# Fetching weights, the second context and the cleared slots of a decoder layer later, with one bias row behind the constants

## The chip, the cores and the metric

The kernel runs on one core of a Trainium2 chip. The metric is the device time of one execution in microseconds. Everything is float32.

## The reference

One decoder layer over 8 batches of 112 tokens with 256 features, with a context of 375 rows per batch:

```python
x = _layernorm(x + attn(x, W1..W4, b1..b4))            # one head: softmax((xW1+b1)(xW2+b2)^T/16)(xW3+b3) W4 + b4
x = _layernorm(x + xattn(x, ctx, mask, ...))           # inside it, three sublayers, each with a residual and a norm:
#   ca = 16-head attention of x over ctx (scores + mask);  x = norm(ca @ co_w + co_b + x) * co_g + co_be
#   sa = 16-head attention of x over x;                    x = norm(sa @ so_w + so_b + x) * so_g + so_be
#   gelu(x @ fi_w + fi_b);                                 x = norm(. @ fo_w + fo_b + x) * fo_g + fo_be
x = _layernorm(x + ffn(x, centroids, gamma, beta, W1, b1, W2, b2))
#   each token goes to the expert (of 8) whose centroid fits best; norm, relu(h W1e^T + b1e) W2e^T + b2e, times alpha
```

## The kernel before, in words

The program is written by hand for five engines, with semaphores. A list, `STEPS`, gives the order of all stages; it is made once from a table of due times, and TensorE (`@block.tensor`), VectorE (`@block.vector`), ScalarE (`@block.scalar`) and GpSimd (`@block.gpsimd`) each walk through it and do their part of every stage. A stage is a pair of name and number. The names that matter here, for batch `u`:

- `aqk`, `as`, `at`, `av`, `ay`: the first attention (queries and keys from `xT_sb[:, u]`, scores, transposed probabilities, values, result). `aw` multiplies W3 by W4 once, so that the output projection is already in the values, and adds b4 to its row: VectorE's line 829, behind `b4_in`. TensorE's projections to a transposed layout are line 488, those to rows line 502.
- `ab`, `ax`: the norm behind it (VectorE, line 878, with the inverse deviation that GpSimd makes) and the transposition of its result (TensorE line 509; VectorE's copy out of PSUM, line 887, which counts up `out_free`).
- `ck`, `cv`: keys (line 495) and values (line 502) of the context; `cq`, `qk`, `cm`, `ct`, `pv`: cross attention's queries, scores, masked exponentials, transpositions, product with the values. VectorE's line 921 adds the mask.
- `sqk`, `sv` and so on: self attention. `f1` (line 656), `f2`: the feed-forward part. `al`, `sc`, `rk`: scattering the tokens to the experts' slots in `x_slots` and `x_more`. After `STEPS` come the experts' tiles (lines 701 to 736).

The steps are ordered by their due times, so for TensorE the first projection of batch 4, (`aqk`, 4), stands between (`ax`, 0) and (`ax`, 1), well before batch 0's first keys. Batch 0 reads `x_first_in`'s part of x, batches 1 to 3 `x_early_in`'s, batches 4 to 7 `x_late_in`'s.

The transfers do not stand in `STEPS`. SP (`@block.sync`) issues most of them in a loop over the batches: context `u`, mask `u`, and at certain `u` something else; from `u` = 2 on, SP first waits until the ring of two context buffers (`out_full`, of `ck` and `cv`) and of two masks (`scores_masked`) is free. In its queue stand also 14 stores of zeros, which clear the slots (`x_slots`, `x_more`), and the experts' weights (`moe`). ScalarE issues seven transfers before its first stage: the b4 row, broadcast; the weights of cross attention; nine more rows; the value biases; the weights of self attention (`wS`); and both feed-forward matrices (`fi_sb`, `fo_sb`). Each transfer raises a semaphore of its own by 16, and the stages wait for it where they first use the data: `w_self` at (`sqk`, 0), `w_ffn` at (`f1`, 0), `zero_in` at (`f1`, 0) and (`al`, 0). GpSimd adds the b4 row to all eight residuals (line 1229), then waits for the other rows and adds two pairs of them (lines 1232, 1233), before it begins with `STEPS`.

Of the kernel before, what the change touches and what calls it, by code (L numbers as in the profile page):

```python
# [12 lines left out]
B, S, D, KX = 8, 112, 256, 375  # L13
# [153 lines left out]
def number(increments):  # L167

    count, before = 0, {}
    for stage in STEPS:  # L170
        if stage[0] in increments:
            before[stage] = count
            count += increments[stage[0]]
    return before, count
# [3 lines left out]
OUT, N_OUT = number(dict(aw=4, aqk=2, av=1, ay=1, ax=1, ck=1, cv=1, cq=1, pv=1, cy=1, cx=1,  # L178
                         sqk=2, sv=1, sy=1, sx=1, f2=1, zx=1, sc=1, rk=1))
# [16 lines left out]
def decoder_layer(nc, xT, xrow, ctxT, mask, weights, fi, fo, cols, rows, vb, b2rows, moe, x_slots, x_more, out):  # L196
    ctx = ExitStack()
    with ctx:
# [3 lines left out]
        def sem(name):  # L202
            return ctx.enter_context(nc.semaphore(name))
# [7 lines left out]
        def take(words):  # L211
            top[0] += words
            assert top[0] <= ARENA, top
            return arena[:, top[0] - words:top[0]]
# [30 lines left out]
        wS = take(4 * C * D).rearrange("p (w c n) -> p w c n", w=4, c=C)  # L245
# [9 lines left out]
        fi_sb = take(C * F).rearrange("p (c f) -> p c f", c=C)  # L255
# [6 lines left out]
        fo_sb = take(FC * D).rearrange("p (f d) -> p f d", f=FC)  # L262
        spread = take(len(ROWS) * D).rearrange("p (r d) -> p r d", r=len(ROWS))
        R = {name: spread[0:S, i] for i, name in enumerate(ROWS)}
# [77 lines left out]
        def col(name, i=0, p=128):  # L342
# [3 lines left out]
        w_first, w_second, w_third, w_cross, w_self, w_ffn = [sem(n) for n in "w_first w_second w_third w_cross w_self w_ffn".split()]  # L346
        consts_in, b4_in, rows_in, v_bias_in, x_first_in, x_early_in, x_late_in, xrow_in, zero_in, moe_b2_in = [sem(n) for n in (
            "consts_in", "b4_in", "rows_in", "v_bias_in", "x_first_in", "x_early_in", "x_late_in", "xrow_in", "zero_in", "moe_b2_in")]
# [50 lines left out]
        def group(n):  # L399

            u, g = divmod(n, NG)
            return u, g, g // 2, g % 2

        def further_tiles(engine, experts=True):

            engine.wait_ge(more_placed, 3)
            loaded = [engine.value_load(tile_expert[0:1, c:c + 1], min_val=0, max_val=E - 1)
                      for c in (*range(EXTRA if experts else 0), EXTRA)]
            return loaded[-1], loaded[:-1]

        def when_used(engine, used, j):


            return engine.If(used > j - E) if j >= E else nullcontext()


        @block.sync
        def _(sp):
            sp.dma_start(xT_sb[:, 0:1], xT[:, 0:1]).then_inc(x_first_in, 16)
            sp.dma_start(wA[:, 0:1], weights[:, 0:1]).then_inc(w_first, 16)  # L420
            sp.dma_start(wA[:, 1:2], weights[:, 1:2]).then_inc(w_second, 16)
            sp.dma_start(consts[:, :], cols).then_inc(consts_in, 16)
            sp.dma_start(xT_sb[:, 1:4], xT[:, 1:4]).then_inc(x_early_in, 16)
            sp.dma_start(wA[:, 2:4], weights[:, 2:4]).then_inc(w_third, 16)
            sp.dma_start(resid[0:S], xrow).then_inc(xrow_in, 16)
            for u in range(B):
                if u >= 2:

                    sp.wait_ge(out_full, 1 + max(OUT["ck", C * (u - 1) - 1], OUT["cv", KC * (u - 1) - 1]))
                sp.dma_start(context[:, u % 2], ctxT[u]).then_inc(ctx_in[u % 2], 16)  # L430
                if u >= 2:

                    sp.wait_ge(scores_masked, H * (u - 1))
                sp.dma_start(masks[0:S, u % 2], mask[u:u + 1].to_broadcast([S, KX])).then_inc(mask_in[u % 2], 16)
                if u == 0:
                    sp.dma_start(xT_sb[:, 4:8], xT[:, 4:8]).then_inc(x_late_in, 16)
                if u == 1:

                    sp.wait_ge(setup, 18)
                    for t in range(TILES):  # L440
                        dst = x_slots[t * 128:(t + 1) * 128, :] if t < E else x_more[(t - E) * 128:(t - E + 1) * 128, :]
                        sp.dma_start(dst, zero[:, t % 2]).then_inc(zero_in, 16)
                if u == B - 2:

                    sp.wait_ge(out_free, OUT["ax", B - 1] + 1)
                    sp.dma_start(moe_w[:, 0], moe[0]).then_inc(moe_in[0], 16)
            sp.wait_ge(out_free, OUT["cy", B - 1] + 1)
            for e in range(1, 5):
                sp.dma_start(moe_w[:, e], moe[e]).then_inc(moe_in[e], 16)
            sp.wait_ge(out_free, OUT["sy", B - 1] + 1)  # L450
            for e in range(5, E):
                sp.dma_start(moe_w[:, e], moe[e]).then_inc(moe_in[e], 16)
            sp.wait_ge(hidden_ready, FIRST_PIECE[-1])
            sp.dma_start(b2_sb.rearrange("p e d -> p (e d)"), b2rows.to_broadcast([128, E * D])).then_inc(moe_b2_in, 16)
            sp.wait_ge(out_free, N_OUT)
            sp.wait_ge(scattered, 16 * B)
            used = None
            for t in range(TILES):
                if t == E:
                    used, _ = further_tiles(sp, experts=False)  # L460
                    sp.wait_ge(more_scattered, 16 * B)
                with when_used(sp, used, t):
                    if t >= 4:
                        sp.wait_ge(t_stats, t - 3)
                    src = x_slots[t * 128:(t + 1) * 128, :] if t < E else x_more[(t - E) * 128:(t - E + 1) * 128, :]
                    sp.dma_start(xs[:, t % 4], src).then_inc(tile_in[t % 4], 16)
# [628 lines left out]
        def _(act):  # L1095
            a = nc.scalar
            act.wait_ge(w_first, 16)
            act.dma_start(R["b4"], rows[:, 0:D].to_broadcast([S, D])).then_inc(b4_in, 16)
            act.dma_start(wC, weights[:, 4:8]).then_inc(w_cross, 16)
            act.dma_start(spread[0:S, 1:].rearrange("p r d -> p (r d)"), rows[:, D:].to_broadcast([S, (len(ROWS) - 1) * D]))\  # L1100
                .then_inc(rows_in, 16)
            act.dma_start(v_bias, vb.unsqueeze(0).to_broadcast([128, 2, D])).then_inc(v_bias_in, 16)
            act.dma_start(wS, weights[:, 8:12]).then_inc(w_self, 16)
            act.dma_start(fi_sb, fi).then_inc(w_ffn, 16)
            act.dma_start(fo_sb, fo).then_inc(w_ffn, 16)
            act.wait_ge(consts_in, 16)
            for stage, i in STEPS:
                kind = stage[0]
# [11 lines left out]
                elif stage == "cm":  # L1120
                    u, at = divmod(i, H)
# [3 lines left out]
                elif stage == "sm":  # L1125
                    u, g, m, h = group(i)
# [227 lines left out]
```

## Time and profile before

| | |
|---|---|
| median of 3 runs | 446.76 us (445.54 to 447.12) |
| profiled execution | 443.95 us, its span 442.1 us |
| TensorE matmul busy | 400.0 us, 90% of the span, 3676 instructions |
| VectorE busy | 273.1 us, 62% |
| ScalarE busy | 241.0 us, 55% |
| GpSimd busy | 127.3 us, 29% |
| mean granted TensorE clock | 0.969 of full |
| DMA | 37.87 MB, of it SP's queue 28.40, ScalarE's 5.60, GpSimd's 3.18 |

The page divides the span into 40 equal slices of 11 us, and gives the busy share of each engine in tenths (9 is 90% or more). A row of the timeline names when an instruction or a run of them began, how long it took in all, its engine and line, what it wrote and read, and in brackets how long the engine was idle just before and what ended that. A float32 matmul shows as two records. SPq and ACTq are the queues on which SP and ScalarE issue DMAs: the duration of such a row is that of the issue, and the time to landing stands in rows of its own.

### The profile page before, as it was taken

What the parts mean: (1) busy time and instruction counts of PE and PEld (TensorE: products, weight loads), DVE (VectorE), ACT (ScalarE), POOL (GpSimd) and SP (SyncE); (2) the same over time, 40 slices, a digit from 0 to 9 for tenths busy, and PEclk for the clock granted to TensorE, in tenths of its full rate; (3) what the DMA queues carried; (4) which work ended last, traced back from release to release, by engine and by line L of the source; (5) the groups of instructions that cost most, each with busy time, mean ns of one, the idle gap of its engine ahead of it and who ended that gap; (6) DMA issues with size and microseconds to landing.
All of it is one profiled execution on the core that took longest, in us unless ns stands there. A gap on an engine that the chain in (4) does not pass through costs nothing.

```text
span 442.1 us, 10512 instructions
## 1 busy us (share of the span) xinstructions
PE 400.0 (90%) x3676; PEld 336.1 (76%) x3676; DVE 273.1 (62%) x945; ACT 241.0 (55%) x822; POOL 127.3 (29%) x256
## 2 busy tenths in 40 slices
PE   5979999999999999999999999999996289998990
PEld 5756787878778778787887887877795189997990
DVE  5476776767676686776777517569677453435432
ACT  0202886588777978779789884855022023332420
POOL 5461102012023031040312205223536325222323
PEclk9999999999999999999999999999998579999996
DMA  7996120010010107000000006920864112111001
GB/s 215 274 362 194 37 51 3 17 36 17 2 36 17 36 2 237 7 18 1 4 0 2 4 1 242 429 93 1 332 262 137 43 49 76 36 37 38 27 13 37
DMA packets 10342, 37.87 MB, mean 86 GB/s; under 512 B 1441, under 2 KB 5777, under 8 KB 8401
## 3 DMA queue, kind: packets, MB, share of 16 engines
q1 hardware_dynamic: 8064, 28.40, 18.7%
q10 hardware_dynamic: 976, 5.60, 3.8%
q0 software_dynamic: 1248, 3.18, 2.2%
q8 instruction: 32, 0.52, 0.5%
q14 instruction: 22, 0.17, 0.1%
HBM read 32.13 MB, written 5.04 MB: 84 GB/s over the span
## 4 chain that ended last, share of the span: by engine, by line
PE 35%; DVE 8%; ACT 4%; issue 3%; POOL 2%; DMA 1%; DVEq 0%; POOLq 0%; ACTq 0%; SPq 0%
PE bank_scores L721 9%; PE bank_out L736 8%; PE bank_out L666 4%; PE bank_pt L656 4%; PE bank_pt L621 2%; PE bank_out L643 2%; PE bank_out L502 1%; ACT arena L1134 1%; DVE stats L797 1%; PE bank_out L488 1%; PE bank_scores L605 1%; DVE arena L921 1%; ACT arena L1123 1%; DVE arena L871 1%; ACT arena L1158 1%
## 5 line engine op out<-in xcount | busy, mean ns | idle before, releaser
L1143 ACT ACTIVATE arena<-bank_pt 125x448 f32<-125x448 f32 (+1 forms) x128 | 67.1, 545 | 37.2 <-PE bank_pt L621 35.2
L1123 ACT ACTIVATE arena<-arena,negmaxc 112x375 f32<-112x375 f32 x128 | 76.9, 604 | 17.2 <-DVE negmaxc L921 16.9
L921 DVE CUSTOM_DVE_ANT_0 arena<-bank_scores,arena 112x375 f32<-112x375 f32 x128 | 65.0, 542 | 19.8 <-PE bank_scores L611 15.3
L621 PE MATMUL bank_pt<-ident,arena 112*125 112x112 f32 (+1 forms) x512 | 74.1, 276 | 1.1 <-ACT arena L1143 0.6
L621 PEld LDWEIGHTS bank_pt<-ident,arena 112*125 112x125 f32 (+1 forms) x512 | 62.9, 175 | 12.7 <-ACT arena L1143 4.5
L502 PE MATMUL bank_out<-arena 128*112 128x256 f32 (+1 forms) x224 | 57.7, 386 | 0.4
L1221 POOL TENSOR_TENSOR vareps<-meanvar,scal 112x1 f32<-112x1 f32 (+1 forms) x50 | 9.9, 198 | 156.0 <-DVE meanvar L800 112.6
L1176 ACT ACTIVATE arena<-bank_scores,consts 128x128 f32<-128x128 f32 x80 | 22.8, 368 | 56.8 <-PE bank_scores L721 56.8
L1134 ACT ACTIVATE arena<-bank_scores,negmaxs 112x112 f32<-112x112 f32 x128 | 43.3, 353 | 6.3 <-DVE negmaxs L927 5.8
L488 PE MATMUL bank_out<-arena 128*128 128x112 f32 x320 | 41.9, 285 | 5.2 <-DMA arena<-weights 4.5
L502 PEld LDWEIGHTS bank_out<-arena 128*112 128x112 f32 (+1 forms) x224 | 37.2, 181 | 10.6 <-issue 2.2
L488 PEld LDWEIGHTS bank_out<-arena 128*128 128x128 f32 x320 | 39.9, 200 | 6.3 <-POOL scal L1192 4.5
L721 PE MATMUL bank_scores<-arena 128*128 128x128 f32 x320 | 39.5, 284 | 0.5 <-DVE arena L1047 0.5
L721 PEld LDWEIGHTS bank_scores<-arena 128*128 128x128 f32 x320 | 38.7, 201 | 0.9 <-issue 0.9
L736 PE MATMUL bank_out<-arena 128*128 128x256 f32 (+1 forms) x160 | 36.0, 379 | 0.0
L736 PEld LDWEIGHTS bank_out<-arena 128*128 128x128 f32 x160 | 29.7, 190 | 3.7
L605 PE MATMUL bank_scores<-arena 32*112 32x375 f32 x256 | 28.8, 518 | 1.8 <-issue 1.8
L666 PE MATMUL bank_out<-arena 128*112 128x256 f32 x128 | 29.2, 381 | 0.4 <-DVE arena L871 0.4
L656 PE MATMUL bank_pt<-arena 128*128 128x224 f32 (+1 forms) x160 | 28.6, 327 | 0.6 <-ACT arena L1158 0.5
L643 PE MATMUL bank_out<-arena 125*32 125x112 f32 (+1 forms) x1024 | 28.7, 260 | 0.5 <-DVE gap L957 0.4
L1224 POOL TENSOR_TENSOR rstd<-vareps,scal 112x1 f32<-112x1 f32 (+1 forms) x50 | 28.0, 560 | 3.9
L1158 ACT ACTIVATE arena<-bank_pt,consts 128x224 f32<-128x224 f32 (+1 forms) x40 | 13.4, 409 | 24.9 <-PE bank_pt L656 24.9
(156 smaller groups left out, 637.2 us busy)
## 6 DMA issues: line engine op xcount, KB each, us to landing
arena<-moe SPq DMA_DIRECT2D x8, 2048.0 KB, 12.7
arena<-ctxT SPq DMA_DIRECT2D x8, 375.0 KB, 3.1
arena<-weights ACTq DMA_DIRECT2D x2, 1024.0 KB, 19.2
arena<-mask SPq DMA_DIRECT2D x8, 164.1 KB, 3.3
x_slots<-arena SPq DMA_DIRECT2D x8, 130.0 KB, 26.3
arena<-x_slots SPq DMA_DIRECT2D x8, 130.0 KB, 2.1
arena<-fi ACTq DMA_DIRECT2D x1, 1024.0 KB, 25.2
arena<-fo ACTq DMA_DIRECT2D x1, 1024.0 KB, 28.1
```

Of the source, the lines that this page charges most:

```text
L488: last = mm(dst[:, m * S:(m + 1) * S], w[:, k, m * 128:(m + 1) * 128], src[:, k], start=k == 0, stop=k == C - 1)
L502: last = mm(dst[0:rows, 0:D], src[:, k], w[:, k], start=k == 0, stop=k == C - 1)
L621: last = nc.tensor.transpose(dst[0:kp, j * S:(j + 1) * S], probs[0:S, (n % 2) * HG + j, c * kp:(c + 1) * kp], ident[0:S, 0:S])
L643: last = mm(dst[32 * j:32 * j + 32, at:at + S], v[:, c, cols:cols + 32], probsT[0:kp, (2 * h + p) % RT, c, j * S:(j + 1) * S], start=p == ...
L656: last = mm(dst[:, at * n:(at + 1) * n], fi_sb[:, k, f * 128:(f + 1) * 128], x3T[:, k, batches[0] * S:batches[0] * S + n], start=k == 0, s ...
L666: last = mm(dst[0:S, 0:D], hiddenT[:, q % 2, f, j * S:(j + 1) * S], fo_sb[:, f], start=f == 0, stop=f == FC - 1)
L721: last = mm(bank[2 * (j % 2) + f // 4][:, f % 4 * 128:(f % 4 + 1) * 128], w1[:, c, f * 128:(f + 1) * 128], xsT[:, j % 2, c], start=c == 0, ...
L736: last = mm(bank[6 + j % 2][:, 0:D], hidT[:, j % 2, f], w2[:, f], start=f == 0, stop=f == FC - 1)
L921: v.tensor_tensor_reduce(out=probsC[0:S, i % (2 * HG)], in0=score_bank[j][0:S, 0:KX], in1=masks[0:S, u % 2], scale=-1.0, scalar=3.0e38, op ...
L1123: a.activation(probsC[0:S, i % (2 * HG)], probsC[0:S, i % (2 * HG)], ACT.Exp, bias=negmax["c"][0:S, u, at:at + 1], scale=-1.0, accum_out=s ...
L1134: a.activation(probsS[0:S, (i % 2) * HG + j], score_bank[j][0:S, SELF_AT:SELF_AT + S], ACT.Exp, bias=negmax["s"][0:S, u, at:at + 1], accum ...
L1143: a.activation(probsT[0:kp, n % RT, c], pt_bank[PT[stage, i] % RP][0:kp, 0:HG * S], ACT.Copy).then_inc(pt_free, 1)
```

## The change

The order of the stages and the sizes stay. Only SP's and ScalarE's DMA issues move:

```diff
             sp.dma_start(consts[:, :], cols).then_inc(consts_in, 16)
+            sp.dma_start(R["b4"], rows[:, 0:D].to_broadcast([S, D])).then_inc(b4_in, 16)
             sp.dma_start(xT_sb[:, 1:4], xT[:, 1:4]).then_inc(x_early_in, 16)
             sp.dma_start(wA[:, 2:4], weights[:, 2:4]).then_inc(w_third, 16)
             sp.dma_start(resid[0:S], xrow).then_inc(xrow_in, 16)
             for u in range(B):
+                if u == 1:
+
+                    sp.wait_ge(out_free, OUT["ax", 0] + 1)
                 if u >= 2:
 
                     sp.wait_ge(out_full, 1 + max(OUT["ck", C * (u - 1) - 1], OUT["cv", KC * (u - 1) - 1]))
...
                 sp.dma_start(masks[0:S, u % 2], mask[u:u + 1].to_broadcast([S, KX])).then_inc(mask_in[u % 2], 16)
-                if u == 0:
+                if u == 1:
                     sp.dma_start(xT_sb[:, 4:8], xT[:, 4:8]).then_inc(x_late_in, 16)
-                if u == 1:
+                    sp.dma_start(wS, weights[:, 8:12]).then_inc(w_self, 16)
+                if u == 2:
 
                     sp.wait_ge(setup, 18)
                     for t in range(TILES):
                         dst = x_slots[t * 128:(t + 1) * 128, :] if t < E else x_more[(t - E) * 128:(t - E + 1) * 128, :]
                         sp.dma_start(dst, zero[:, t % 2]).then_inc(zero_in, 16)
+                if u == 3:
+                    sp.dma_start(fi_sb, fi).then_inc(w_ffn, 16)
+                    sp.dma_start(fo_sb, fo).then_inc(w_ffn, 16)
...
             act.wait_ge(w_first, 16)
-            act.dma_start(R["b4"], rows[:, 0:D].to_broadcast([S, D])).then_inc(b4_in, 16)
             act.dma_start(wC, weights[:, 4:8]).then_inc(w_cross, 16)
...
             act.dma_start(v_bias, vb.unsqueeze(0).to_broadcast([128, 2, D])).then_inc(v_bias_in, 16)
-            act.dma_start(wS, weights[:, 8:12]).then_inc(w_self, 16)
-            act.dma_start(fi_sb, fi).then_inc(w_ffn, 16)
-            act.dma_start(fo_sb, fo).then_inc(w_ffn, 16)
             act.wait_ge(consts_in, 16)
```

SP's queue, from the eighth of its transfers on, before (`ctxT` is a context, `xT` of 896 elements the x of batches 4 to 7, both in the big tile `arena`):

```order
L430 DMA arena<-ctxT 128x750
L434 DMA arena<-mask 112x375
L436 DMA arena<-xT 128x896
L430 DMA arena<-ctxT 128x750
L434 DMA arena<-mask 112x375
L442 DMA x_slots<-arena 128x260 [waits setup]
L442 DMA x_slots<-arena 128x260 x7
L442 DMA x_more<-arena 128x260 x6
L430 DMA arena<-ctxT 128x750 [waits out_full]
```

and the same place of the change:

```order
L434 DMA arena<-ctxT 128x750
L438 DMA arena<-mask 112x375
L434 DMA arena<-ctxT 128x750 [waits out_free]
L438 DMA arena<-mask 112x375
L440 DMA arena<-xT 128x896
L441 DMA arena<-weights 128x2048
L434 DMA arena<-ctxT 128x750 [waits out_full]
L438 DMA arena<-mask 112x375 [waits scores_masked]
L447 DMA x_slots<-arena 128x260 [waits setup]
L447 DMA x_slots<-arena 128x260 x7
L447 DMA x_more<-arena 128x260 x6
```

The x of batches 4 to 7 has moved behind the second context and mask, and these stand behind a wait for `out_free`, of which nothing stood there before; the stores have moved behind the third context and mask.

ScalarE's queue before its first exponential (`rows` of 256 elements is b4), before:

```order
L1098 DMA arena<-rows 112x256 [waits w_first]
L1099 DMA arena<-weights 128x2048
L1100 DMA arena<-rows 112x2304
L1102 DMA arena<-vb 128x512
L1103 DMA arena<-weights 128x2048
L1104 DMA arena<-fi 128x2048
L1105 DMA arena<-fo 128x2048
```

and of the change:

```order
L1106 DMA arena<-weights 128x2048 [waits w_first]
L1107 DMA arena<-rows 112x2304
L1109 DMA arena<-vb 128x512
```

Four transfers have gone from it to SP. TensorE's rows are the same before and after; where it meets the moved x, they read:

```order
L509 MATMUL bank_out<-ident,xrows 128x112 [waits out_free,norm_done]
L509 MATMUL bank_out<-ident,xrows 128x112
L488 MATMUL bank_out<-arena 128x112 [waits out_free,x_late_in]
L488 MATMUL bank_out<-arena 128x112 x3
L488 MATMUL bank_out<-arena 128x112 [waits out_free]
L488 MATMUL bank_out<-arena 128x112 x3
```

The first two are (`ax`, 0), whose copy SP now waits for, the others (`aqk`, 4).

## Rows read from the trace of the kernel before

**Rows 1.** The page's 40 slices: TensorE's and the DMA engines' busy tenths.

```profile
PE   5979999999999999999999999999996289998990
...
DMA  7996120010010107000000006920864112111001
```

**Rows 2.** Stretches: length, busy time of each engine, granted clock, DMA share, GB/s.

```profile
20.00:30.00 10.00, 7.66 (x46) 5.49 (x44) 7.25 (x23) 0.86 (x4) 7.26 (x14) 1.00 1.01 319
```

**Rows 3.** TensorE's waits up to 60 us: total, times, longest.

```profile
PE bank_out L488 <- DMA arena<-weights: 4.5, 1, 4.5
```

**Rows 4.** Timeline of GpSimd: start, duration, what, idle time before.

```profile
17.44 5.51 POOL L1229 TENSOR_TENSOR arena<-arena 112x256 f32<-112x256 f32 x8 [10.96 <-DVE minus_centroids L830]
24.98 0.72 POOL L1232 TENSOR_TENSOR arena<-arena 112x256 f32<-112x256 f32 x1 [2.02 <-DMA arena<-rows]
```

**Rows 5.** Timeline of VectorE: first norm of batch 0, copy of its transposition.

```profile
27.84 0.41 DVE L878 TENSOR_SCALAR xrows<-arena,meanvar,rstd 112x256 f32<-112x256 f32 x1
...
30.34 0.38 DVE L887 COPY arena<-bank_out 128x224 f32<-128x224 f32 x1
```

**Rows 6.** SP's issues on the timeline; then issues by size, with us to landing.

```profile
0.80 0.39 SPq L419 DMA_DIRECT2D arena<-xT  x1
...
2.66 0.43 SPq L423 DMA_DIRECT2D arena<-xT  x1
...
7.90 13.37 SPq L442 DMA_DIRECT2D x_slots<-arena  x7
...
arena<-xT SPq DMA_DIRECT2D x1, 448.0 KB, 20.7
arena<-xT SPq DMA_DIRECT2D x1, 336.0 KB, 4.4
```

**Rows 7.** Timeline of TensorE: sixteen projection records with and without DMA traffic.

```profile
20.65 2.04 PE L488 MATMUL bank_out<-arena 128*128 128x112 f32 x16
...
58.95 1.95 PE L488 MATMUL bank_out<-arena 128*128 128x112 f32 x16
```

**Rows 8.** Timeline of TensorE: the first projections of batch 4.

```profile
29.59 2.33 PE L488 MATMUL bank_out<-arena 128*128 128x112 f32 x16 [0.68 <-DVE arena L868]
```

**Rows 9.** The context's issue and landing; SP's later timeline; a single large transfer.

```profile
L430 SPq DMA_DIRECT2D arena<-ctxT x8: 328/330/949, 4.1 to 174.7; - x8
...
DMA to landing us min/median/max: 2.8/3.1/23.1
...
56.97 0.82 SPq L430 DMA_DIRECT2D arena<-ctxT  x1
79.06 0.33 SPq L434 DMA_DIRECT2D arena<-mask  x1
...
arena<-b2rows SPq DMA_DIRECT2D x1, 1024.0 KB, 5.1
```

**Rows 10.** Around idle times of TensorE: timeline, stretches (columns as rows 2), chain.

```profile
339.85 0.54 PE L680 MATMUL bank_out<-chosen,ones 112*112 112x8 f32 x2 [2.19 <-DVE chosen L969]
...
352.00:356.00 4.00, 1.18 (x5) 0.72 (x5) 1.80 (x7) 0.00 (x0) 0.00 (x0) 0.50 0.51 133
4.50:8.40 3.90, 3.90 (x18) 3.90 (x19) 1.29 (x4) 0.00 (x0) 1.91 (x13) 1.00 0.87 260
...
355.94 5.88 PE L721 MATMUL bank_scores<-arena 128*128 128x128 f32 x32 [0.49 <-DVE arena L1047]
...
362.03 3.57 PE bank_scores L721 x32
```

**Rows 11.** First uses on TensorE: self attention, fourth and fifth context, feed-forward.

```profile
79.85 1.95 PE L488 MATMUL bank_out<-arena 128*128 128x112 f32 x16
97.90 1.44 PE L495 MATMUL bank_out<-arena 128*128 128x375 f32 x4
129.74 1.43 PE L495 MATMUL bank_out<-arena 128*128 128x375 f32 x4
...
L656 PE MATMUL bank_pt<-arena x160: 275/352/457, 252.7 to 333.4; 128*128 128x224 f32 x96, 128*128 128x112 f32 x64
```

## The prediction

> **What bounds the kernel now.** I read the page's slices first [rows 1]: TensorE is at nine tenths or more from the fourth slice to the thirty-first, so the matmul queue sets the pace, except at the start and around 350 us. The DMA engines are nearly full in the first three slices and mostly idle afterwards, up to the late ones. Second the stretch in which both meet, 20 to 30 us [rows 2]: DMA share 1.01 at 319 GB/s, and TensorE idle for 2.3 of 10 us. Does the full DMA system hold the matmuls up? The waits of TensorE answer it [rows 3]: the only DMA that it waited for up to 60 us is the first weight, 4.5 us, and that one is issued before any that the change moves. The other waits there are for VectorE and ScalarE, the latency chain of the first attention. On GpSimd one wait ends with a DMA, 2.02 us for the broadcast rows [rows 4].
>
> **What could be gained.** The crowd at the start is hardly on the path. With the rows in sooner, GpSimd's two additions would follow its eight residual additions at 22.95 (17.44 + 5.51) instead of 24.98 [rows 4]. But what VectorE takes from GpSimd next, the first normalisation at 27.84, shows no idle time before it [rows 5]: VectorE came from other work. I count 0. b4 is moved ahead and away from ScalarE's crowd, so it lands sooner; nobody waited for it: 0. It pushes the second to fourth inputs back by one issue, 0.43 us, from 2.66 + 4.4 = 7.1 to 7.5 us [rows 6]. They are needed by the seventeenth projection matmul; 18 ran in the first 3.9 us from 4.50 [rows 10], so at 8.0: 0 again, though by only 0.5. ScalarE loses four issues that lie before its first exponential, which waits for VectorE: 0. Only slowing by traffic is left. Sixteen projection matmuls took 2.04 us in the crowd and 1.95 with an idle DMA system [rows 7]; 4.6% of the 26 us up to 30.7 is 1.2 us at the most, on a chain that is mostly latency. I take 0.
>
> **What is lost: batch 4's input.** The fetch of x for batches 4 to 7 landed 20.7 us after its issue [rows 6], in time: TensorE didn't wait for it [rows 3]. Now SP first waits for VectorE's copy of the first transposed batch (ax of batch 0), which runs from 30.34 to 30.72 [rows 5]; then it issues the second context, its mask, and only then this x. TensorE's order is unchanged, and in it the first projection of batch 4 stands directly behind that same transposition: it started at 29.59 [rows 8]. The transfer is now asked for after it is needed.
>
> When does it land? An issue takes 0.33 us [rows 9]: context at 30.8, mask 31.1, x 31.5. With 375 and 164 KB ahead of its own 448 KB, 987 KB must move. Lower end: x as if alone, 31.5 plus the 3.1 us of a context of 375 KB [rows 9], 34.6. Upper end: the pace at which the start moved its first 1,033 KB, 6.3 us from 0.80 to 7.1 [rows 6], so 6.0 us: 36.8. Nearest is a single transfer of 1,024 KB on an idle system, 5.1 us [rows 9]; scaled 5.0, so 35.8. The stall at batch 4's projection is 35.8 - 29.59 = **6.2 us**, between 5.0 and 7.2. Everything behind it on TensorE waits, among it the first keys, queries and scores, and with them VectorE, ScalarE and GpSimd, which have nothing else to do meanwhile but two normalisations. As TensorE then runs without gaps for 28 slices [rows 1], nothing takes the shift back.
>
> In sentences apart: the Trainium skill, page "DMA: Bandwidth & Descriptors", section "Anatomy of one DMA — SWDGE (gpsimd) path", gives one DMA a fixed 2.0 us plus its bytes over 436 GB/s; by that, 987 KB take an estimated 4.3 us, the stall is 5.5, and the sum below 7.1 instead of 7.8. The same rule makes 4.4 us of the 1,024 KB that took 5.1 here [rows 9]; the row decides.
>
> **What is lost: the clock.** After 2.19 us of idling TensorE's matmuls of eight columns took 0.54 us a pair; the granted clock from 352 to 356 is 0.50, which is 1.2 GHz, and the next 32 matmuls took 5.88 us where 32 like them took 3.57 later: 2.3 us for one restart [rows 10]. At the start of the kernel the granted clock reads 1.00, yet 18 matmuls took 3.9 us where 16 take 1.95 later, so 1.7 us more than such 18 would [rows 7, 10]. A stall of 6.2 us behind a stretch with 2.3 us of idling in ten [rows 2] should drop the clock to 1.2 GHz too. I take **2.1 us**, nearer to the restart after an idle time; the ends are 0 and 2.3.
>
> **Given back.** Batch 4's sixteen matmuls are now spread over 2.33 us instead of 1.95 and wait 0.68 for VectorE [rows 8]. In a stall VectorE catches up, and at half the clock it has longer for its part. At most 0.7, at least 0.3; I take **0.5**.
>
> **The other moves.** The second context lands before x and is used after it: 0. Self-attention weights: 1,024 KB behind x, in by about 40; first used at 79.85 [rows 11]: 0. The 14 clearing stores move from 7.90 to behind the third mask, where the next issue stood at 56.97, with the shift 65; beside other traffic the first seven took 13.37 us to issue [rows 6], so fourteen 26.7. Behind them in SP's queue stands the fourth context: issued by 92, landed by 95, needed at 97.90 + 8 = 106 [rows 9, 11]: hidden with 11 us to spare. Both feed-forward weights go behind the fourth mask, issued at 79.06 before [rows 9]; their 2,048 KB take about twice 5.1 us, to 98 with the shift. The fifth context, behind them, is used at 129.74 and the feed-forward begins at 252.7 [rows 11]. All 0. A cover that fails there would show as a DMA wait of TensorE at one of these places.
>
> **Sum.** 6.2 + 2.1 - 0.5 = **+7.8 us**. The profiled execution took 443.95 (span 442.1, 1.85 around it), 2.8 below the median of the three runs, 446.76. On its own time that makes 451.8; on the median, **454.6**. The mechanism's own bounds are 5.0 + 1.7 - 0.7 = 6.0 and 7.2 + 2.3 - 0.3 = 9.2, so 452.8 to 456.0.
>
> **Rivals.** That the change doesn't do what it says is out: the rows of the four compute engines are the same in the same order, but for ScalarE's DMA issues.
> - *The clock stays up.* For it: 2.3 us of gaps between 20 and 30 us left it at 1.00 [rows 2]. Against: the pair behind 2.19 us of idling [rows 10]. It gives 6.2 - 0.4 = 5.8: 452.6.
> - *The self weights share the engines with x.* If the 1,024 KB issued behind x move beside it, x lands with all 2,011 KB; at 2.0 us per 649 KB (5.1 less 3.1, [rows 9]) that is 3.1 us later. +10.9: 457.7. Against: the second to fourth inputs landed 4.4 us after their issue, though over a megabyte was queued right behind [rows 6].
> - *The stores hold the fourth context.* It decides if the fourteen take more than 37 us; at 3 us each, 42, the fourth keys wait 5 more: +13: 460. Against: 1.9 each in the worst company [rows 6].
> - *The other side: relief at the start.* The copy that releases SP comes earlier, because rows and traffic no longer hold anybody up. Only what pulls that copy forward counts, and all of it does; from 30.7 it would have to move to 22.9 to make up for 7.8. The rows allow 2.0 [rows 4] and 1.2, so +4.6: 451.4. For the sign to turn, most of the first attention's latency would have to be waiting for DMA behind the names of other engines; then, with 9 us of relief, 445.6.
>
> **How the numbers follow.** Forecast 0.78 (454.6); clock stays up 0.09 (452.6); weights share 0.05; stores 0.03; relief that cancels the loss 0.05, of which 0.03 ends within the bound and 0.02 beyond. A measurement of this kernel can tell about 0.5%, 2.2 us, from no change. So slower 0.95, same 0.03, faster 0.02. The range goes from 450.5, under the quiet clock with partial relief, to 458.0, above the shared weights. The stores and full relief are left out, 8 in 100, and some of the forecast's own tail: three runs alone span 1.6 us.
>
> **What would show it.** The waits of TensorE up to 60 us have a second DMA entry, for x, of 5 to 7 us, at the first projection behind the first transposition; the sixteen matmuls of batch 4 take about 4 us instead of 2.33; SP's next issue after the first mask stands at about 30.8; no later wait of TensorE ends with a DMA. GpSimd's wait for the rows is gone, and nothing is faster for it. I am wrong if there is no such wait, or if it is there and the end moves by less than 4 us: then later stages had slack that I don't see.

## The result, and the profile of the changed kernel

The changed kernel takes 458.99 us (median of 4, 458.41 to 464.32), the kernel before beside it 446.94 (445.54 to 447.52): ratio 1.0301, 95% interval 1.0221 to 1.0381. That is 12.0 us slower where 7.8 had been forecast, and 1.0 us above the top of the range. The profiled execution took 459.31 us with a span of 457.4. The ratios, here and below, go by means and not by medians: they leave out runs more than 1.5% above the fastest of their kernel, and here the run of 464.32 us raises the mean.

The page's slices of the changed kernel, to be set beside [rows 1]; the line between is the granted TensorE clock in tenths. One slice is 11.4 us:

```profile
PE   4964999999999999999999899999997288998990
...
PEclk9895999999999999999999999999999569999997
DMA  7905017061001011500000003940674122010001
```

The crowd of transfers is gone after the second slice, and the fourth slice, busy to nine tenths before, is busy to four tenths and at half the clock. From the fifth on, the picture is the old one. TensorE's waits say by whom, where [rows 3] had one line:

```profile
PE bank_out L496 <- DMA arena<-xT: 10.6, 2, 8.7
...
PE bank_out L496 <- DMA arena<-weights: 4.6, 1, 4.6
```

Two waits for x instead of the one that was forecast. TensorE's timeline has both in place (L496 is L488 of before):

```profile
4.57 3.64 PE L496 MATMUL bank_out<-arena 128*128 128x112 f32 x16 [4.57 <-DMA arena<-weights]
10.07 2.58 PE L496 MATMUL bank_out<-arena 128*128 128x112 f32 x16 [1.86 <-DMA arena<-xT]
...
31.69 0.35 PE L517 MATMUL bank_out<-ident,xrows 112*128 112x112 f32 x2
40.80 3.75 PE L496 MATMUL bank_out<-arena 128*128 128x112 f32 x16 [8.75 <-DMA arena<-xT]
44.34 0.58 PE L517 MATMUL bank_out<-ident,xrows 112*128 112x112 f32 x2
...
45.53 1.48 PE L503 MATMUL bank_out<-arena 128*128 128x375 f32 x4
```

At 10.07, batch 1's projection starts 1.9 us after the end of batch 0's. At 40.80 it is batch 4's projection, which stood at 29.59 [rows 8]. Before, batches 0 and 1 made one unbroken run of 32 records, and the first keys stood at 32.79:

```profile
4.50 5.80 PE L488 MATMUL bank_out<-arena 128*128 128x112 f32 x32 [4.50 <-DMA arena<-weights]
...
32.79 1.50 PE L495 MATMUL bank_out<-arena 128*128 128x375 f32 x4
```

SP's queue of the change and the landings behind it:

```profile
3.13 0.43 SPq L424 DMA_DIRECT2D arena<-xT  x1
...
33.88 0.33 SPq L434 DMA_DIRECT2D arena<-ctxT  x1
34.25 0.43 SPq L438 DMA_DIRECT2D arena<-mask  x1
34.72 0.43 SPq L440 DMA_DIRECT2D arena<-xT  x1
35.20 0.43 SPq L441 DMA_DIRECT2D arena<-weights  x1
...
arena<-weights SPq DMA_DIRECT2D x1, 1024.0 KB, 8.0
...
arena<-xT SPq DMA_DIRECT2D x1, 448.0 KB, 6.0
arena<-xT SPq DMA_DIRECT2D x1, 336.0 KB, 6.9
```

x of batches 1 to 3 landed 6.9 us after an issue at 3.13, so at 10.0; in [rows 6] it was 2.66 + 4.4 = 7.1. x of batches 4 to 7 landed at 34.72 + 6.0 = 40.7. VectorE's copy of (`ax`, 0), for which SP waits, came 3.1 us later than the 30.34 of [rows 5]:

```profile
33.47 0.38 DVE L895 COPY arena<-bank_out 128x224 f32<-128x224 f32 x1
```

The clock, in stretches (length, busy times, granted clock, DMA share, GB/s):

```profile
36.00:40.00 4.00, 0.00 (x0) 0.00 (x0) 0.00 (x0) 0.00 (x0) 0.00 (x0) 0.50 0.91 241
40.00:44.00 4.00, 3.20 (x15) 3.20 (x16) 0.67 (x2) 0.00 (x0) 0.00 (x0) 0.50 0.47 198
44.00:48.00 4.00, 3.80 (x20) 2.83 (x20) 2.11 (x6) 0.00 (x0) 0.00 (x0) 0.81 0.01 2
```

From 36 to 40 us no engine does anything, and TensorE resumes at a granted clock of 0.50, which is 1.2 GHz. GpSimd no longer waits for the rows, where it had waited 2.02 us [rows 4], and nothing behind it is sooner for that: VectorE's first norm began at 30.97 us, 3.1 later than before like everything around it.

```profile
26.03 0.72 POOL L1236 TENSOR_TENSOR arena<-arena 112x256 f32<-112x256 f32 x1
```

Against before, the first keys start at 45.53 instead of 32.79, 12.7 us later, and this distance stays: the feed-forward matmuls

```profile
L664 PE MATMUL bank_pt<-arena x160: 274/352/457, 265.4 to 346.1; 128*128 128x224 f32 x96, 128*128 128x112 f32 x64
```

run from 265.4 to 346.1, where they ran from 252.7 to 333.4 [rows 11]. The two spans differ by 15.3 us; the last 2.6 arise among the experts' tiles, in a gap of 1.01 us and smaller ones for which the profile shows no cause. The medians differ by 12.0 only.

### The profile page after: what moved, and what is told of

It reads as the page before. It is cut to its first block, busy times and chain, and to the rows that moved or that the text cites. A ratio compares the mean times of both kernels' runs of the same rounds, so it can differ in the third digit from the quotient of the medians.

```text
span 457.4 us, 10512 instructions
## 1 busy us (share of the span) xinstructions
PE 403.8 (88%) x3676; PEld 339.7 (74%) x3676; DVE 273.4 (60%) x945; ACT 240.8 (53%) x822; POOL 127.4 (28%) x256
## 4 chain that ended last, share of the span: by engine, by line
PE 33%; DVE 7%; ACT 4%; issue 3%; DMA 2%; POOL 2%; DVEq 0%; POOLq 0%; ACTq 0%; SPq 0%
PE bank_scores L729 9%; PE bank_out L744 7%; PE bank_out L674 4%; PE bank_pt L664 4%; PE bank_pt L629 2%; PE bank_out L651 2%; PE bank_out L510 1%; ACT arena L1138 1%; DVE stats L805 1%; PE bank_out L496 1%; PE bank_scores L613 1%; DVE arena L929 1%; ACT arena L1127 1%; DVE arena L879 1%; DMA out<-arena,tile_token 1%
## 5 line engine op out<-in xcount | busy, mean ns | idle before, releaser
L929 DVE CUSTOM_DVE_ANT_0 arena<-bank_scores,arena 112x375 f32<-112x375 f32 x128 | 65.1, 543 | 19.8 <-PE bank_scores L619 15.3
L496 PE MATMUL bank_out<-arena 128*128 128x112 f32 x320 | 44.2, 295 | 15.2 <-DMA arena<-xT 10.6
L496 PEld LDWEIGHTS bank_out<-arena 128*128 128x128 f32 x320 | 42.0, 210 | 16.2 <-DMA arena<-xT 11.0
L510 PEld LDWEIGHTS bank_out<-arena 128*112 128x112 f32 (+1 forms) x224 | 37.3, 181 | 10.6 <-issue 2.4
L744 PEld LDWEIGHTS bank_out<-arena 128*128 128x128 f32 x160 | 29.7, 190 | 3.6
```

The costliest lines, as they stand in the source:

```text
L496: last = mm(dst[:, m * S:(m + 1) * S], w[:, k, m * 128:(m + 1) * 128], src[:, k], start=k == 0, stop=k == C - 1)
L510: last = mm(dst[0:rows, 0:D], src[:, k], w[:, k], start=k == 0, stop=k == C - 1)
L744: last = mm(bank[6 + j % 2][:, 0:D], hidT[:, j % 2, f], w2[:, f], start=f == 0, stop=f == FC - 1)
L929: v.tensor_tensor_reduce(out=probsC[0:S, i % (2 * HG)], in0=score_bank[j][0:S, 0:KX], in1=masks[0:S, u % 2], scale=-1.0, scalar=3.0e38, op ...
```

## The experiments

All times are medians beside the kernel before on the same chip. Before itself took 444.7 to 448.4 us there, so I compare distances to before. Every row and every landing comes from one execution of its kernel. "x early" is x of batches 1 to 3, "x late" that of batches 4 to 7. Waits are in us.

**Taking the two losses apart.** `b4_only` is the kernel before with

```diff
+            sp.dma_start(R["b4"], rows[:, 0:D].to_broadcast([S, D])).then_inc(b4_in, 16)
             sp.dma_start(xT_sb[:, 1:4], xT[:, 1:4]).then_inc(x_early_in, 16)
...
-            act.dma_start(R["b4"], rows[:, 0:D].to_broadcast([S, D])).then_inc(b4_in, 16)
```

> The kernel before with only the b4 row moved: from ScalarE's queue to SP's, behind the constants and ahead of x of batches 1 to 3. Theory A (the move alone delays x of batches 1 to 3 from 7.1 to about 10.0 us after the start, and everything behind it): 3.1 us slower than before, TensorE waits 1.9 us for x at its second batch, (ax, 0) is copied at about 33.5. Theory B (the prediction: the move only costs one issue, 0.43 us, and is covered; what came late in the change came from the other moves): within 0.5 us of before.

`after_b4_back` is the change with these lines undone.

> The change, but b4 again as the first transfer of ScalarE. Theory A: 3.1 us faster than the change, the copy of (ax, 0) at 30.3, the stall for x of batches 4 to 7 as long as before at 8 us or a little more. Theory B: no faster than the change.

`after_x_back` is the change with x late where it was:

```diff
-                if u == 1:
+                if u == 0:
                     sp.dma_start(xT_sb[:, 4:8], xT[:, 4:8]).then_inc(x_late_in, 16)
+                if u == 1:
                     sp.dma_start(wS, weights[:, 8:12]).then_inc(w_self, 16)
```

> The change, but x of batches 4 to 7 again behind the first mask, ahead of SP's wait. Theory A (the stall of 8.7 us at batch 4 and the slow clock behind it are 9.5 us of the 12.7): 9.5 us faster than the change, some 3.1 over before. Rival (later moves cost something too, the rest of the 15 us between the two profiled executions): 5 us or more over before.

`after_both_back` has both undone.

> The change without its two losses: b4 on ScalarE and x of batches 4 to 7 behind the first mask; second context, self-attention and feed-forward weights and stores stay late. Theory A: within 1 us of before, since nobody waited for the crowd at the start. Rival (relief at the start): 1 to 3 us faster than before. Rival (a late transfer costs): 2 us or more slower than before.

| kernel | median | before beside it | ratio, 95% interval | wait for x early | wait for x late |
|---|---|---|---|---|---|
| change | 458.99 | 446.94 | 1.0301 (1.0221 to 1.0381) | 1.86 | 8.75 |
| after_b4_back | 457.05 | 448.35 | 1.0175 (1.0108 to 1.0243) | none | 8.21 |
| after_x_back | 450.75 | 448.35 | 1.0037 (0.9997 to 1.0077) | 3.79 | none |
| b4_only | 451.0 | 448.35 | 1.0051 (1.0012 to 1.0090) | 4.47 | none |
| after_both_back | 448.76 | 448.35 | 0.9985 (0.9957 to 1.0014) | none | none |

The late x alone costs 8.7 us, b4 alone 2.4 to 2.7 (the interval of b4_only excludes no change, that of after_x_back just includes it); together that is some 11, the change's 12. With both undone nothing is left that these runs can tell from no change: neither a cost of the later context, weights and stores, nor a gain from relieving the start. b4_only's wait is the plainest row against my 0, but from an execution of 457.80 us, the slowest of its ten:

```profile
12.09 3.76 PE L489 MATMUL bank_out<-arena 128*128 128x112 f32 x16 [4.47 <-DMA arena<-xT]
```

**Why b4 costs.** The expectations below name two candidates. Theory A1: b4's small rows, ahead of x early in the same queue, hold it up; but 112 KB should not take 3 us by themselves (an estimate: 448 KB landed in 3.3 in after_x_first, below). Theory A2: at the head of ScalarE's queue b4 had been a brake. It needed 10.8 us to land there, against 4.0 to 5.0 on SP ahead of x, and only behind it could the 1,024 KB of cross-attention weights compete with SP's queue. Its row of before:

```profile
arena<-rows ACTq DMA_DIRECT2D x1, 112.0 KB, 10.8
```

`b4_behind_x` moves b4 to SP, but one place further back:

```diff
             sp.dma_start(xT_sb[:, 1:4], xT[:, 1:4]).then_inc(x_early_in, 16)
+            sp.dma_start(R["b4"], rows[:, 0:D].to_broadcast([S, D])).then_inc(b4_in, 16)
```

> The kernel before with b4 on SP, but behind x of batches 1 to 3 instead of ahead of it. Theory A1 (small rows of b4 ahead in the same queue hold x up): x lands 4.4 us after its issue as before, TensorE does not wait for it, time as before. Theory A2 (b4 had been a brake at the head of ScalarE's queue: as soon as it is gone, the large cross-attention weights start at 4.4 us and take their share from x): x takes 6.5 us or more from its issue although nothing new stands ahead of it, TensorE waits 1.5 us or more, the time is 2 to 3 us over before.

x early took 5.1 us and TensorE didn't wait for it. But the next transfer in the queue, W3 and W4, took 13.7 us instead of 7.4, and TensorE waited for that:

```profile
17.39 3.78 PE L536 MATMUL bank_out<-arena 128*128 128x256 f32 x8 [3.57 <-DMA arena<-weights]
```

This row too is from the slowest of ten executions, 452.11 us. The median is 447.46 beside 444.68, ratio 1.0036 (1.0000 to 1.0072), so a cost is likely but hardly clear of noise. The form that I had given theory A2 fails in this execution (x early was not late), and A1 doesn't account for it: the delay struck what stood *behind* b4 and x. `b4_only_act_waits` adds to b4_only:

```diff
+            act.wait_ge(x_early_in, 16)
             act.dma_start(wC, weights[:, 4:8]).then_inc(w_cross, 16)
```

> b4_only (b4 on SP ahead of x of batches 1 to 3), and ScalarE issues its first transfer, the cross-attention weights, only when that x has landed. Theory A1: x still lands late, at 9.5 us or later. Theory A2: x lands at about 7.0 us, as nothing competes with it, TensorE does not wait for it, and the time is that of before or a little less.

x early took 5.5 us (it landed at 8.6, between the 7.0 of theory A2 and the 9.5 of A1), the wait shrank to 0.40, W3 and W4 took 7.6; 446.64 beside 444.68, ratio 1.0028 (0.9994 to 1.0062). The most direct test is `b4_twice`: b4 is fetched by SP ahead of x early, *and* ScalarE still fetches the same row first, to an unused place:

```diff
+            sp.dma_start(R["b4"], rows[:, 0:D].to_broadcast([S, D])).then_inc(b4_in, 16)
             sp.dma_start(xT_sb[:, 1:4], xT[:, 1:4]).then_inc(x_early_in, 16)
...
-            act.dma_start(R["b4"], rows[:, 0:D].to_broadcast([S, D])).then_inc(b4_in, 16)
+            act.dma_start(hiddenT[0:S, 0].rearrange("p f n -> p (f n)")[:, 0:D], rows[:, 0:D].to_broadcast([S, D])).then_inc(b4_again, 16)
```

(ScalarE also waits for `b4_again` before it first uses that place.) `b4_only_2` and `act_waits_2` are b4_only and b4_only_act_waits once more, beside it.

> b4_only, and ScalarE still issues a copy of the b4 row first (into a place that is free until the feed-forward), ahead of the cross-attention weights: the slow small transfer stays at the head of its queue. Theory A2 (b4's place at the head of ScalarE's queue kept the large weights away from x of batches 1 to 3 and from W3 and W4): x lands 5 to 5.5 us after its issue, W3 and W4 within 8, and the kernel is within 1 us of before and faster than b4_only_2 beside it. Theory A1 (the small rows ahead of x in SP's own queue): x takes 6.5 us or more as in b4_only, and the time is that of b4_only_2.

> b4_only once more, beside the other two on the same chip: x of batches 1 to 3 takes 6.5 to 9 us from its issue, 2 us slower than before by both theories.

> b4_only_act_waits once more, beside the other two. Theory A2: as b4_twice, within 1 us of before. Theory A1: as b4_only_2.

First the second row of ScalarE's queue on the timeline of b4_twice and, among the landings, both b4 rows and x early:

```profile
4.55 0.46 ACTq L1101 DMA_DIRECT2D arena<-weights  x1
...
arena<-weights SPq DMA_DIRECT2D x1, 512.0 KB, 6.9
...
arena<-xT SPq DMA_DIRECT2D x1, 336.0 KB, 4.9
...
arena<-rows SPq DMA_DIRECT2D x1, 112.0 KB, 4.2
arena<-rows ACTq DMA_DIRECT2D x1, 112.0 KB, 10.0
```

With the brake in place, x early lands at 3.13 + 4.9 = 8.0, and TensorE's run is unbroken again:

```profile
4.20 6.38 PE L490 MATMUL bank_out<-arena 128*128 128x112 f32 x32 [4.20 <-DMA arena<-weights]
```

All kernels with x early at the start, by the time at which ScalarE issues the large weights (it waits for the first weight's landing), one execution each:

| b4 | kernel | large weights issued at | x early, us to landing | W3, W4, us to landing |
|---|---|---|---|---|
| on SP ahead of x | b4_only | 3.83 | 8.9 | 16.2 |
| | after_x_back | 4.00 | 8.4 | 14.3 |
| | after_ws_later | 4.27 | 6.2 | 7.8 |
| | after_warm | 4.29 | 6.5 | 9.2 |
| | b4_only_2 | 4.48 | 6.2 | 8.1 |
| | change | 4.50 | 6.9 | 8.4 |
| | after_x_first | 4.51 | 5.8 | 7.5 |
| | b4_only_act_waits | 8.72 | 5.5 | 7.6 |
| | act_waits_2 | 8.96 | 5.7 | 7.5 |
| on SP behind x | b4_behind_x | 4.09 | 5.1 | 13.7 |
| on both | b4_twice | 4.55 | 4.9 | 6.9 |
| head of ScalarE's queue | warm_tail | 4.57 | 6.0 | 7.9 |
| | warm_front | 4.60 | 5.2 | 7.2 |
| | after_both_back | 4.71 | 4.4 | 7.4 |
| | warm_both | 4.77 | 4.3 | 7.3 |
| | before | 4.90 | 4.4 | 7.4 |
| | after_b4_back | 4.94 | 4.7 | 7.7 |

The three executions in which the large transfer was issued by 4.09 are the ones whose W3 and W4 took 13.7 to 16.2 us, against 6.9 to 9.2 in all others; two of the three are the slowest executions of their kernels, after_x_back's is not. From 4.27 on, there is no such order left: with b4 on SP ahead of x, x early took 5.8 to 6.9 us at whichever time, and 5.5 and 5.7 where ScalarE held its transfers back. Against that stand 4.3 to 6.0 in the six executions with b4 at the head of ScalarE's queue and 4.9 in b4_twice. So the rows fit both theories, with about a microsecond for each, but the groups overlap and single executions scatter by as much: how the loss divides between b4's place ahead of x and the brake that is gone is not shown.

Nor do the medians of the last three kernels decide it: b4_twice 448.7, b4_only_2 450.73, act_waits_2 450.23, beside 447.56 (ratios 1.0017, 0.9981 to 1.0052; 1.0024, 0.9982 to 1.0065; 1.0032, 0.9996 to 1.0069). b4_twice is the nearest to before, as theory A2 said; act_waits_2 is about as far off as b4_only_2, as A1 said, and not as near as b4_twice, as A2 had it; no distance is clear of noise. (x early took 6.2 us in b4_only_2, a little less than the 6.5 to 9 expected.)

**What a wait costs here.** A wait in this place can cost much more than its length. In b4_only_2 TensorE waited 1.06 us, and the sixteen records behind took 3.75 us, as they do at a granted clock of 0.50 (40.80 in the change); batch 4's projection came at 33.47, in b4_twice at 29.87. In b4_only_act_waits 0.40 us of waiting was enough, and the first keys stood at 35.66, in b4_twice, without a wait, at 33.07. In warm_tail (below; like before, up to this point) TensorE waited 0.95 us, but the next sixteen took 2.04 and the keys stood at 33.26:

```profile
9.34 3.75 PE L489 MATMUL bank_out<-arena 128*128 128x112 f32 x16 [1.06 <-DMA arena<-xT]
```

```profile
8.68 3.76 PE L489 MATMUL bank_out<-arena 128*128 128x112 f32 x16 [0.40 <-DMA arena<-xT]
...
35.66 1.50 PE L496 MATMUL bank_out<-arena 128*128 128x375 f32 x4
```

```profile
8.72 2.04 PE L488 MATMUL bank_out<-arena 128*128 128x112 f32 x16 [0.95 <-DMA arena<-xT]
```

So a good part of what b4's move costs is TensorE's slow start going on for longer, and whether it does varies from execution to execution. The change itself lay between: 2.58 us for the sixteen behind its wait of 1.86, and a granted clock of 0.50 from 12 to 14 us.

**What makes the late x late.** `after_x_first` issues it first behind SP's wait:

```diff
                 if u == 1:
 
                     sp.wait_ge(out_free, OUT["ax", 0] + 1)
+                    sp.dma_start(xT_sb[:, 4:8], xT[:, 4:8]).then_inc(x_late_in, 16)
...
                 if u == 1:
-                    sp.dma_start(xT_sb[:, 4:8], xT[:, 4:8]).then_inc(x_late_in, 16)
                     sp.dma_start(wS, weights[:, 8:12]).then_inc(w_self, 16)
```

> The change, but x of batches 4 to 7 is the first transfer behind SP's wait, ahead of the second context and mask. If the stall is latency plus the bytes ahead in the queue: x lands 3.5 us after its issue at 33.9, at 37.4 instead of 40.7, and the kernel is 3 us faster than the change. If the self-attention weights behind it are what slows it: x still takes 5 to 6 us, and the gain is 1 to 1.5 us.

`after_ws_later` moves the weights that stood right behind it:

```diff
                 if u == 1:
                     sp.dma_start(xT_sb[:, 4:8], xT[:, 4:8]).then_inc(x_late_in, 16)
-                    sp.dma_start(wS, weights[:, 8:12]).then_inc(w_self, 16)
                 if u == 2:
+                    sp.dma_start(wS, weights[:, 8:12]).then_inc(w_self, 16)
```

> The change, but the self-attention weights are issued behind the third mask instead of right behind x of batches 4 to 7. If they share the engines with x: x lands 1 us or more sooner (5.0 instead of 6.0 us after its issue), 1 us faster than the change. If the queue serves in its order: x takes 5.3 to 6 us as in the change, and the time is the change's.

Landing and wait of x late, in after_x_first and then in after_ws_later:

```profile
arena<-xT SPq DMA_DIRECT2D x1, 448.0 KB, 3.3
...
36.89 3.76 PE L496 MATMUL bank_out<-arena 128*128 128x112 f32 x16 [5.13 <-DMA arena<-xT]
```

```profile
arena<-xT SPq DMA_DIRECT2D x1, 448.0 KB, 4.4
...
38.85 3.76 PE L495 MATMUL bank_out<-arena 128*128 128x112 f32 x16 [7.11 <-DMA arena<-xT]
```

In front, x takes 3.3 us; behind context and mask, without the weights behind it, 4.4 from its issue or 5.2 from the context's at 33.57; with the weights behind it 6.0 and 6.8 in the change. From its own issue it was 5.5 in after_b4_back and 5.3 in after_warm, where the weights stood behind it too. So a transfer that was queued *later* seems to cost 0.9 to 1.6 us, with a single execution on the side without it. The medians go the same way: 452.05 beside 444.68, +7.4 (1.0172, 1.0092 to 1.0251), and 455.73 beside 445.14, +10.6 (1.0241, 1.0168 to 1.0314), against +12.0 of the change (1.0221 to 1.0381). The intervals overlap, the last two by most of their width, so the weights' share rests on the landings.

**The clock behind the stall.** `after_warm` lets TensorE do needless matmuls where it would wait:

```diff
                 if stage == "aqk":
...
+                    if i == 4:
+                        for n in range(32):
+                            mm(score_bank[0][:, 0:S], W["W1"][:, n % 2, 0:128], xT_sb[:, 0, n % 2], start=True, stop=True)
                     pe.wait_ge(x_first_in if i == 0 else x_early_in if i < 4 else x_late_in, 16)
```

> The change, and TensorE runs 32 needless matmuls (7.8 us, into a bank that nobody reads yet) in front of batch 4's projection, where it otherwise idles 8.7 us. If the idle time costs clock behind it: batch 4's sixteen records take 2.3 instead of 3.75 us and the keys behind start 1.5 to 2 us earlier; 1.5 to 2 us faster than the change. If the clock is not it: no difference, or slower.

```profile
32.90 7.31 PE L528 MATMUL bank_scores<-arena 128*128 128x112 f32 x64
41.11 2.04 PE L496 MATMUL bank_out<-arena 128*128 128x112 f32 x16 [0.90 <-DMA arena<-xT]
...
44.26 1.50 PE L503 MATMUL bank_out<-arena 128*128 128x375 f32 x4
```

From batch 4's projection to the first keys it is 3.15 us instead of the 4.73 of the change (40.80 to 45.53): the clock costs 1.6 us there. The median, 455.74 beside 444.68, is +11.1, 1.0 less than the change's distance where 1.5 to 2 had been expected (1.0235, 1.0170 to 1.0300, which overlaps the change's interval).

**The clock in the kernel before.** after_both_back's profiled execution had no DMA wait, and yet its first keys stood at 34.69 and took 2.81 us instead of 1.50:

```profile
28.00:32.00 4.00, 2.42 (x14) 2.01 (x14) 3.32 (x12) 0.00 (x0) 2.41 (x6) 0.90 0.00 0
32.00:36.00 4.00, 3.80 (x14) 2.87 (x14) 1.78 (x5) 0.00 (x0) 1.37 (x2) 0.50 0.84 187
```

The clock fell behind the first attention, whose gaps of 0.90 and 0.67 us are the kernel's own: before's profiled execution had the same ones and stayed at 1.00. `warm_front`, `warm_tail` and `warm_both` are the kernel before with `ident` times `ident` into a score bank where TensorE idles:

```diff
+            def spin(n, bank, w=ident, src=ident):
+                for _ in range(n):
+                    mm(bank[:, 0:128], w[:, :], src[:, :], start=True, stop=True)
             pe.wait_ge(setup, 1)
+            spin(6, score_bank[0])
+            extra = {("ay", 0): 2, ("ay", 2): 2, ("ay", 3): 3, ("aqk", 4): 2, ("aw", 0): 0}
+            extra.update({("rk", 6): 6, ("zx", 7): 4, ("sc", 7): 3, ("rk", 7): 4})
             for stage, i in STEPS:
+                spin(extra.get((stage, i), 0), score_bank[0])
...
             mm(bank[7][:, 0:E], ones[0:S, :], chosen[0:S, B - 1], start=True, stop=True).then_inc(totals, 1)
+            spin(22, score_bank[0])
```

(warm_front has the first `spin` and the first table, warm_tail the second table and the last `spin`.)

> The kernel before, and TensorE multiplies the identity by itself where it would idle up to 30 us: six times before its first weight has landed, two or three times in four gaps of the first attention. Nothing of the change is in it. If the kernel's spread from 443.5 to 449.5 us is a clock that in some executions falls in those gaps, and the start is at half clock: 1 to 2 us faster than before and no execution with a clock below 0.965. Rival (the clock is only a mark of slow executions): no difference, or slower by the needless work.

> The kernel before, and TensorE multiplies the identity by itself in the gaps of the last routing steps (17 times) and while it waits 6.2 us for the experts' first rows (22 times). If a restart costs what the first expert's matmuls showed (5.88 against 3.57 us) and the routing's small matmuls run at half clock too: 2.3 to 4 us faster than before. Rival (the needless work delays the routing): no gain.

> Both kinds of needless matmuls together in the kernel before: 3 to 6 us faster than before, the mean granted clock above 0.99. Rival as with its parts.

| kernel | median | before beside it | ratio, 95% interval | granted clock |
|---|---|---|---|---|
| warm_front | 443.52 | 445.14 | 0.9962 (0.9925 to 0.9999) | 0.966 to 0.973 |
| warm_tail | 445.22 | 445.14 | 1.0009 (0.9976 to 1.0043) | 0.976 to 0.987 |
| warm_both | 441.70 | 445.14 | 0.9910 (0.9873 to 0.9948) | 0.981 to 0.988 |

warm_both is the fastest of all: 3.4 us under before and, from distance to distance, some 15 under the change; its granted clock stayed under the 0.99 that I had expected. The 32 records of its first expert, against 5.88 us in [rows 10]:

```profile
354.59 3.81 PE L730 MATMUL bank_scores<-arena 128*128 128x128 f32 x32 [0.67 <-DVE arena L1056]
```

Of the 25 executions of before in this group, 21 lie between 443.1 and 445.8 us at granted clocks of 0.965 to 0.973, four between 449.2 and 449.4 at 0.959; warm_front has none of the latter kind in ten, which is too few to rule them out. warm_tail alone missed its 2.3 to 4 us. Its first expert took 3.81 us too, but began 324.5 us behind the first keys, where before, warm_front and warm_both have 323.0 to 323.2. In that one execution the time is lost between GpSimd's last scatter (issued at 349.42) and SP's load of the slots (353.66): 4.24 us, against 2.68 in before and in warm_both. Why, and why the two together give more than their sum, stays open.

## Why the prediction was wrong, step by step

- **The bound**: right. TensorE sets the pace, and relieving the crowd at the start brought nothing that can be measured (after_both_back: 0.9985); from 45.53 to 346.1 the shift stayed at 12.7 us. I had misread the slices by one, nine tenths end at the thirtieth, which changes nothing. Every 0 of "the other moves" held for its own cover, since no later wait of TensorE ended with a DMA. The 14 stores, for which I had allowed 26.7 us, were issued in 7.3.
- **The late x**: right in mechanism, place and sign. The term was 6.2 us and measured 8.1 (40.80 against 29.59 + 3.13), beyond its own bound of 7.2. The 5.0 us for 987 KB were right without the weights behind (5.2 in after_ws_later); with them it was 6.2 to 6.8 in three executions. The rival "the self weights share the engines" had this with a chance of 0.05 and a price of 3.1; it measured 0.9 to 1.6, in one execution each. What was wrong is its "against": that the second to fourth inputs landed in 4.4 us with over a megabyte queued behind. A short time doesn't show that it would not have been shorter with nothing behind. By the Trainium skill, page "DMA: Bandwidth & Descriptors", section "Anatomy of one DMA — SWDGE (gpsimd) path", the 987 KB take an estimated 4.3 us. That fit is stated for GpSimd's transfers and these were SP's; the measured 5.2 lies above it, and the 5.0 from the row was nearer.
- **The clock and what is given back**: 2.1 - 0.5 = 1.6 us forecast; the trace shows 12.7 - 3.1 - 8.1 = 1.5, after_warm 1.6. The difference is right; no run measured its two terms apart.
- **b4**: this is the step that failed, "0 again, though by only 0.5", and the larger miss: 3.1 us in the trace (the copy of (ax, 0) at 33.47, not 30.34), 2.4 to 2.7 in the medians. x early landed at 10.0 us, not at 7.5. I costed the move at the issue that it adds in SP's queue: neither at the time that b4's own rows take ahead of x, nor at what it sets free in ScalarE's queue, the large weights behind it; the runs show that the move costs, and leave open how it divides between the two. A row that could have warned me was b4's own landing before, 112 KB in 10.8 us, which I had left out. And with only 0.5 us of cover, a price for missing it belonged into the range, with the slow matmuls behind it: a wait of 0.40 us came with keys 2.6 us later.
- **The base**: the distance from median to median was 12.0, from the trace's terms 12.7. The profiled execution of before lies 2.8 us under its median, and its granted clock stayed at 1.00 up to 36 us, where that of after_both_back fell; that others of its executions have such a fall is likely but not shown.
- **Range and chances**: slower at 0.95 was right; the top of 458.0 lacked b4's 2.4 us. With it, the forecast would have been 457.0 and the range, moved up by as much, would have held the result.

## What to carry to other kernels

Moving a transfer off a queue also moves everything that stood behind it there: look up how long it took, and ask who may compete when it is gone. The late x, asked for in time, cost nothing here even in a crowd; made to wait for a sign that comes after its first use, it cost its whole latency, the bytes ahead of it and, as the landings suggest, part of those behind. A cover of half a microsecond is no cover: price what happens if it fails. Where TensorE idles for the sake of others, the clock can be lost too, and needless matmuls in such gaps were worth 0.9% here.

## What the runs showed of the hardware that I had not expected

- 112 KB of one row, broadcast to 112 partitions, took 10.0 to 11.1 us at the head of ScalarE's queue while SP's queue was busy (seven executions), 4.0 to 5.0 on SP's queue ahead of x early and 7.6 behind it.
- With 1,024 KB issued 0.48 us *behind* it on the same queue, a transfer of 448 KB landed 5.3 to 6.0 us after its issue, without them 4.4 (three executions against one).
- Waits of 0.40 and 1.06 us ahead of the second batch were followed by sixteen records in 3.76 and 3.75 us, the time that they take at 1.2 GHz, while in b4_twice 32 in one run took 6.38 in all. The profile gives all of them a granted clock of 1.00, so at the start of this kernel the durations tell more than that column.
- The granted clock can fall to 0.50 behind gaps of 0.9 and 0.67 us with no DMA wait at all (after_both_back, 32 to 36 us); behind the same gaps it stayed at 1.00 in before's profiled execution.
